# Attention of a four-layer graph kernel: the head sums of the softmax made by another engine and another operation

## The reference

```python
q = (x @ Wq + bq).reshape(N, H, HEAD)   # k and v likewise
scores = jnp.einsum('nhd,mhd->nhm', q, k) / np.sqrt(HEAD)
scores = jnp.where(adj[:, None, :] == 0, -1000000000.0, scores)
attn = jax.nn.softmax(scores, axis=1)
attn_out = jnp.einsum('nhm,mhd->nhd', attn, v).reshape(N, D_OUT)
attn_out = attn_out @ Wo + bo
h1 = _layer_norm(x + attn_out, g1, be1)
```

## Time and profile before

| | before |
|---|---|
| median of 3 runs | 468.87 us (468.62 to 468.89) |
| profiled execution | 468.27 us, span 466.5 us |
| granted TensorE clock, mean | 0.996 |
| TensorE matmuls | 449.2 us busy, 96% of the span |
| VectorE | 310.3 us, 67% |
| ScalarE | 191.1 us, 41% |
| GpSimd | 150.9 us, 32% |
| the chain that ended last | PE 80%, DVE 12% |

### The profile page before, as it was taken

One profiled execution on the slowest core, in us unless ns is written; L12 is line 12 of the kernel. 1 busy time (PEld: TensorE's weight loads), 2 busy tenths in 40 slices (PEclk: granted clock), 3 DMA queues, 4 the chain that ended last, 5 costly groups with the idle time before them and its releaser, 6 DMA issues.

```text
span 466.5 us, 5948 instructions
## 1 busy us (share of the span) xinstructions
PE 449.2 (96%) x2108; PEld 328.3 (70%) x2108; DVE 310.3 (67%) x571; ACT 191.1 (41%) x266; POOL 150.9 (32%) x101
## 2 busy tenths in 40 slices
PE   8999999979899999899999999999999999999997
PEld 3456544434458888678878888888888888888766
DVE  5999868999997998943875836252353237133865
ACT  5898834546124440352632262134303332227240
POOL 5000033212111954464243444044434444344100
PEclk9999999999999999899999999999999999999999
DMA  8870007600000555145020222223221342020002
GB/s 280 173 282 1 1 2 161 109 1 0 1 1 1 139 155 202 24 73 199 1 83 8 91 90 91 90 90 115 90 91 31 118 139 74 22 90 1 0 1 91
DMA packets 24203, 37.49 MB, mean 80 GB/s; under 512 B 5744, under 2 KB 6256, under 8 KB 24176
## 3 DMA queue, kind: packets, MB, share of 16 engines
q1 hardware_dynamic: 21728, 32.80, 21.0%
q0 software_dynamic: 2160, 4.19, 5.3%
q10 hardware_dynamic: 288, 0.13, 0.1%
HBM read 36.07 MB, written 1.05 MB: 80 GB/s over the span
## 4 chain that ended last, share of the span: by engine, by line
PE 80%; DVE 12%; issue 3%; ACT 2%; DVEq 1%; DMA 1%; POOL 0%
PE ps L1257 17%; PE ps L1258 17%; PE ps L1259 17%; PE ps L1319 5%; PE ps L1330 4%; PE ps L1286 3%; PE ps L1285 3%; DVE rsum L963 2%; PE ps L1407 2%; PE ps L1312 2%; DVE e_sb L399 2%; DVE one_src L844 1%; DVE stats L770 1%; PE ps L1270 1%; PE ps L1403 1%
## 5 line engine op out<-in xcount | busy, mean ns | idle before, releaser
L481 POOL TENSOR_TENSOR w_lo<-w_stage,w_hi 128x1024 fp32r<-128x1024 f32 x21 | 52.0, 2477 | 134.1 <-ACT w_hi L567 124.2
L567 ACT ACTIVATE w_hi<-w_stage 128x2048 fp32r<-128x2048 f32 x22 | 42.0, 1909 | 53.4 <-PE ps L1259 53.4
L482 POOL TENSOR_TENSOR w_lo<-w_stage,w_hi 128x1024 fp32r<-128x1024 f32 x21 | 55.2, 2631 | 0.0
L1257 PE MATMUL ps<-w_hi,hid_hi 128*128 128x512 f32 x112 | 43.6, 389 | 0.0
L1258 PE MATMUL ps<-w_lo,hid_hi 128*128 128x512 f32 x112 | 43.6, 389 | 0.0
L1259 PE MATMUL ps<-w_hi,hid_lo 128*128 128x512 f32 x112 | 43.6, 389 | 0.0
L1257 PE MATMUL ps<-T_hi,w_hi 128*128 128x512 f32 (+1 forms) x108 | 39.3, 364 | 0.0
L1259 PE MATMUL ps<-T_hi,w_lo 128*128 128x512 f32 (+1 forms) x108 | 38.6, 358 | 0.0
L1258 PE MATMUL ps<-T_lo,w_hi 128*128 128x512 f32 (+1 forms) x108 | 38.6, 357 | 0.0
L1157 DVE TENSOR_SCALAR tmp<-ps,bl 128x512 f32<-128x512 f32 x16 | 12.0, 749 | 39.9 <-ACT hid_hi L721 39.9
L505 POOL TENSOR_TENSOR rstd<-vareps,scalars 128x1 f32<-128x1 f32 x24 | 16.3, 680 | 61.9 <-DVE vareps L772 61.9
(11 more groups left out here) (239 smaller groups left out, 1013.8 us busy)
## 6 DMA issues: line engine op xcount, KB each, us to landing
w_stage<-in_L_gnn_Wr SPq DMA_DIRECT2D x8, 1024.0 KB, 5.1
w_stage<-in_L_gnn_Wl SPq DMA_DIRECT2D x8, 1024.0 KB, 5.3
w_stage<-in_L_gnn_W SPq DMA_DIRECT2D x5, 1024.0 KB, 5.8
x_sb<-in_x SPq DMA_DIRECT2D x4, 256.0 KB, 3.7
w_q<-in_L_gnn_Wq SPq DMA_DIRECT2D x1, 1024.0 KB, 7.2
w_k<-in_L_gnn_Wk SPq DMA_DIRECT2D x1, 1024.0 KB, 9.7
w_v<-in_L_gnn_Wv SPq DMA_DIRECT2D x1, 1024.0 KB, 5.6
w_o<-in_L_gnn_Wo SPq DMA_DIRECT2D x1, 1024.0 KB, 10.6
```

The lines of the kernel that those rows point to most:

```text
L481: gp.tensor_tensor(w_lo[h][:, 0:2], stage[s][:, 0:2], f32(w_hi[h][:, 0:2]), ALU.subtract)
L482: gp.tensor_tensor(w_lo[h][:, 2:4], stage[s][:, 2:4], f32(w_hi[h][:, 2:4]), ALU.subtract)\
L567: nc.scalar.activation(w_hi[home(u)][:], stage[u % 2][:], ACT.Copy).then_inc(hi_made, 1)
L1257: nc.tensor.matmul(goal, a_hi, b_hi, start=start, stop=False, **kw)
```

## The change

It is confined to the attention.

- GpSimd makes two additions a step, from step 1 on: for each group of 4 heads, heads 0, 1 plus heads 2, 3. It writes them to `pair_sums[i % 2]`, laid out 256 columns by 4 sums, so that one operation's outputs for one head lie 4 floats apart.
- VectorE sums the 4 neighbours of each column with one `tensor_reduce` (`head_sum`). Step 0 stays as it was.
- VectorE's order in a step becomes maxima i+1, product of i-1, sum of i, reciprocal of i.
- The exponentials lie in 4 buffers, and TensorE takes the values of step i-3 at step i, in the places where those of i-2 stood (at step 2 there are none).
- Behind the steps TensorE takes values 5, output tiles 0 and 1, values 6, values 7, and then the first 8 transposes of the count matrix (`count_transposes`), which stood ahead of values 7. `attended_out(0)` on ScalarE moves from step 5 to step 6. The products of step 6 are one operation instead of two.

```diff
--- before.py
+++ after.py
@@ -101,7 +101,7 @@
     k_sb = place("k_sb", [P, PAIRS, N], F32, rQK + MAT)
     v_sb = place("v_sb", [P, NT, D], F32, rQK + 2 * MAT)
     half_sum = place("half_sum", [P, HEADS // 2, HN], F32, rQK + 3 * MAT)
-    pool_sum = place("pool_sum", [P, HEADS // 4, HN], F32, rQK + 3 * MAT + 4 * HN * 4)
+    pair_sums = [place(f"pair_sum{i}", [P, HN, HEADS // 2], F32, rQK + 3 * MAT + (1 - i) * 4 * HN * 4) for i in range(2)]
     ff_hi = place("ff_hi", [P, FT, N], F32R, rQK)
     ff_lo = place("ff_lo", [P, FT, N], F32R, rQK + 2 * MAT)
     R_hi = place("R_hi", [P, NT, D], F32R, rQK)
@@ -111,7 +111,7 @@
 
 
 
-    E_BUFS = 3
+    E_BUFS = 4
     e_bufs = [place(f"e_sb{i}", [P, HEADS, HN], F32, rVZ + i * MAT) for i in range(E_BUFS)]
     c_hi = place("c_hi", [P, NT, N], F32R, rVZ)
     c_lo = place("c_lo", [P, NT, N], F32R, rVZ + MAT)
@@ -283,7 +283,7 @@
         inner_made, part_made, edge_cast, weight_made = (sem("inner_made"), sem("part_made"), sem("edge_cast"),
                                                          sem("weight_made"))
         first_half = sem("first_half")
-        sums_made, rinv_made, pool_half = sem("sums_made"), sem("rinv_made"), sem("pool_half")
+        sums_made, rinv_made, pairs_made = sem("sums_made"), sem("rinv_made"), sem("pairs_made")
         dve = sem("dve")
         pool = sem("pool")
         ln_var = sem("ln_var")
@@ -528,12 +528,14 @@
             add_row("L0_gnn_be2", x_sb, be2_added)
             gp.wait_ge(tr_done, tr_no(T0, NT - 1))
             add_row("L0_gnn_bo", h_sb, bo_added)
-            for i in range(DIRECT, STEPS):
-
-                e = e_bufs[i % E_BUFS]
-                gp.wait_ge(exp_done, 2 * i + 1)
-                gp.wait_ge(sums_made, i)
-                gp.tensor_tensor(pool_sum[:], e[:, 0:2], e[:, 2:4], ALU.add).then_inc(pool_half, 1)
+            for i in range(1, STEPS):
+
+                e, pairs = e_bufs[i % E_BUFS], pair_sums[i % 2]
+                gp.wait_ge(sums_made, max(i - 1, 1))
+                for g in range(2):
+                    gp.wait_ge(exp_done, 2 * i + g + 1)
+                    gp.tensor_tensor(pairs[:, :, 2 * g:2 * g + 2].rearrange("p n h -> p h n"), e[:, 4 * g:4 * g + 2],
+                                     e[:, 4 * g + 2:4 * g + 4], ALU.add).then_inc(pairs_made, 1)
             rstd_of(LN1)
             gp.wait_ge(h_ready, NT)
             split_lo(W1B)
@@ -660,7 +662,7 @@
                     coarse_scores(1, 0)
                 if DIRECT <= i + 1 < STEPS:
                     coarse_scores(i + 1, 1)
-                if i == NT + 1:
+                if i == NT + 2:
                     attended_out(0)
                 if i + 2 < STEPS:
                     coarse_scores(i + 2, 0)
@@ -932,11 +934,10 @@
 
             maxima(0)
             values_in(1)
-            for i in range(STEPS):
-                e = e_bufs[i % E_BUFS]
-                if i == 1 or DIRECT < i < STEPS - 1:
-                    maxima(i + 1)
-                r = rsum[:, i % 2, :]
+
+            def head_sum(i):
+
+                e, r = e_bufs[i % E_BUFS], rsum[:, i % 2, :]
                 if i == 0:
                     v.wait_ge(exp_done, 1)
                     nc.vector.tensor_tensor(half_sum[:, 0:2], e[:, 0:2], e[:, 2:4], ALU.add).then_inc(first_half, 1)
@@ -944,31 +945,42 @@
                     link(nc.vector.tensor_tensor(half_sum[:, 2:4], e[:, 4:6], e[:, 6:8], ALU.add))
                     v.wait_ge(first_half, 1)
                     link(nc.vector.tensor_tensor(half_sum[:, 0:2], half_sum[:, 0:2], half_sum[:, 2:4], ALU.add))
-                elif i < DIRECT:
-                    v.wait_ge(exp_done, 2 * (i + 1))
-                    link(nc.vector.tensor_tensor(half_sum[:], e[:, 0:4], e[:, 4:8], ALU.add))
-                    link(nc.vector.tensor_tensor(half_sum[:, 0:2], half_sum[:, 0:2], half_sum[:, 2:4], ALU.add))
+                    nc.vector.tensor_tensor(r, half_sum[:, 0], half_sum[:, 1], ALU.add).then_inc(sums_made, 1)
                 else:
-                    v.wait_ge(exp_done, 2 * (i + 1))
-                    link(nc.vector.tensor_tensor(half_sum[:, 0:2], e[:, 4:6], e[:, 6:8], ALU.add))
-                    v.wait_ge(pool_half, i - DIRECT + 1)
-                    link(nc.vector.tensor_tensor(half_sum[:, 0:2], half_sum[:, 0:2], pool_sum[:], ALU.add))
-                nc.vector.tensor_tensor(r, half_sum[:, 0], half_sum[:, 1], ALU.add).then_inc(sums_made, 1)
-                if i == 0:
-                    maxima(1)
-                    values_in(2)
-                if i == 1:
-                    values_in(3)
+                    v.wait_ge(pairs_made, 2 * i)
+                    nc.vector.tensor_reduce(r, pair_sums[i % 2][:], AX_X, ALU.add).then_inc(sums_made, 1)
+
+            def head_inverse(i):
+
+                r = rsum[:, i % 2, :]
                 v.wait_ge(sums_made, i + 1)
                 nc.vector.reciprocal(r, r).then_inc(rinv_made, 1)
-                if i == 1:
-                    maxima(DIRECT + 1)
+
+            def normalised(i):
+
                 v.wait_ge(rinv_made, i + 1)
-                if i < STEPS - 2:
+                if i < STEPS - 1:
                     probabilities(nc.vector, i, slice(0, HEADS)).then_inc(prob_done, 2)
                 else:
                     probabilities(nc.vector, i, slice(0, HEADS // 2)).then_inc(prob_done, 1)
                     probabilities(nc.vector, i, slice(HEADS // 2, HEADS)).then_inc(prob_done, 1)
+
+            head_sum(0)
+            maxima(1)
+            values_in(2)
+            head_inverse(0)
+            normalised(0)
+            maxima(2)
+            head_sum(1)
+            values_in(3)
+            head_inverse(1)
+            for i in range(2, STEPS):
+                if i + 1 < STEPS:
+                    maxima(i + 1)
+                normalised(i - 1)
+                head_sum(i)
+                head_inverse(i)
+            normalised(STEPS - 1)
 
 
             g1_row, be1_row = wait_row(GAMMA1), wait_row(BETA1)
@@ -1436,25 +1448,18 @@
             values_part(1, 3)
             values_part(2, 0, 1)
             for i in range(STEPS):
-                if i == STEPS - 1:
-
-                    pe.wait_ge(raw_in["o"], 16)
-                    pe.wait_ge(exp_done, 2 * STEPS - 2)
-                    plain_rows_tile(wo_bank(0), 0, att_sb, w_o, wo_done)
                 centre(i, 0)
                 centre(i, 1)
                 if i == 0:
                     scores(1, 0)
                 if i == 1:
                     values_part(3, 1)
-                if i == 2:
+                if i >= 3:
+                    values(i - 3, 0)
+                if i + 1 < STEPS:
                     scores(i + 1, 1)
-                if i >= 2:
-                    values(i - 2, 0)
-                if i + 1 < STEPS and i != 2:
-                    scores(i + 1, 1)
-                if i >= 2:
-                    values(i - 2, 1)
+                if i >= 3:
+                    values(i - 3, 1)
                 if i + 2 < STEPS:
                     scores(i + 2, 0)
                 if i == 0:
@@ -1462,9 +1467,13 @@
                     values_part(3, 0)
                 if i == 1:
                     values_part(3, 2, 3)
+            values(STEPS - 3, 0)
+            values(STEPS - 3, 1)
+            pe.wait_ge(raw_in["o"], 16)
+            plain_rows_tile(wo_bank(0), 0, att_sb, w_o, wo_done)
+            plain_rows_tile(wo_bank(1), 1, att_sb, w_o, wo_done)
             values(STEPS - 2, 0)
             values(STEPS - 2, 1)
-            plain_rows_tile(wo_bank(1), 1, att_sb, w_o, wo_done)
 
             def count_transposes(src, bank, s, done):
 
@@ -1473,10 +1482,10 @@
                 last.then_inc(done, 1)
 
             pe.wait_ge(exp_done, 2 * STEPS)
+            values(STEPS - 1, 0)
+            values(STEPS - 1, 1)
             for s in C_ROWS[:2]:
                 count_transposes(ct_hi, s, s, c_tr)
-            values(STEPS - 1, 0)
-            values(STEPS - 1, 1)
             pe.wait_ge(att_made, 2)
             plain_rows_tile(wo_bank(2), 2, att_sb, w_o, wo_done)
             for t in range(NT // 2):
```

## The result

| | before | after |
|---|---|---|
| median (runs) | 468.76 us (4; 468.62 to 468.89) | 464.67 us (4; 464.59 to 464.84) |
| profiled execution | 468.27 us, span 466.5 | 464.84 us, span 463.0 |
| ratio | 1 | 0.9918, 95% interval 0.9907 to 0.9929 |

The change is 4.1 us faster. In the profiled executions the difference is 3.43 us. The third output tile, by which the prediction measures the attention, starts at 130.85 instead of 134.03, 3.18 earlier. The first matmul of the next part shifts by the same (142.35 to 139.17). VectorE's last operation starts 3.15 earlier (463.65 to 460.50). So the attention made the gain, and the work behind it handed it on.

A forecast was written before the change was run, and what follows sets the result against it. VectorE was taken to bound the attention's steps (7.36 us, to become 6.53); with step 1's loss and the tail, the third output tile starts 2.2 us earlier: 468.9 - 2.2 = 466.7 us, own range 466.2 to 467.2, full range 465.0 to 472.5.

The forecast's parts named there:

- What bounds the kernel: Attention steps from step 3 on: VectorE limits at 7.36 us a step, the loop without its queue needing 6.33.
- the exclusion: Two-input operations of VectorE and GpSimd exclude each other and take turns; VectorE's one-input reduction and reciprocal take no part.
- X: Time of one GpSimd pair sum with strided output: taken as 1.27 to 1.46 us, at most 2.40.
- Rival 1: GpSimd's pair sums are slow: break-even at X = 1.65, 470.4 us at 1.8, about 476.5 at 2.40; chance 0.27.
- a slow reduction: VectorE's new reduction taking 2.28 us instead of 1.22 would make steps of 7.59 and 470.8 us.
- VectorE's step: Attention from step 3 on: maxima 1.39, product 2.21, reduction 1.26, reciprocal 1.67, together 6.53 us instead of 7.36.
- Step 1: Two pair sums collide with product 0 and maxima 2, making the centring of step 2 1.25 us later.
- Rival 2: Nothing is lost in step 1, so 1.25 us comes back: 465.4 us; chance 0.10.
- The tail: From the last centring to the third output tile, TensorE works without idle time for 16.74 us; tile starts at 131.81.
- Taking the difference from the median: The 2.2 us gain, reckoned on the profiled 468.27, was subtracted from the runs' median, giving 468.9 - 2.2 = 466.7 us.

The follow-up runs named there:

- experiment 3: New kernel with VectorE's product of step i again behind the reciprocal of step i; 474.12 us, 1.0115 to the old kernel.
- experiment 4: New kernel with a third GpSimd pair sum in each step (group 0's made twice); 471.27 us, 1.0063 to the old kernel.
- experiment 5: New kernel with pair sums written head by head, contiguous, so VectorE's reduction reads four values 1 KB apart; 468.83 us, 1.0003 to the old kernel.
- experiment 1: New kernel with step 1's sum made by VectorE alone, GpSimd's pair sums beginning at step 2; 464.00 us, 0.9907 to the old kernel.
- second measurement: The new kernel unchanged, timed again beside the old one: 464.79 us (5 runs) against 468.57 (9 runs), 0.9922.
- experiment 10: Old kernel with the new tail of TensorE's queue and ten matmuls filling the gap ahead of the last centring; 468.96 us, 1.0012 to the old kernel.
- experiment 11: Old kernel with the first group's scores of step 5 computed twice, to fill TensorE's gap at step 4; 468.32 us, 0.9994 to the old kernel.
- experiment 8: New kernel with output tile 0 put back ahead of the last centring; 465.54 us, 0.9935 to the old kernel.
- experiment 9: Old kernel with only the tail of TensorE's queue as in the new one; 470.23 us beside 468.51, 1.0034.

## Why the prediction was right in direction and too small

**What bounds the kernel, and the exclusion: right.** VectorE was the limit of each step from step 3 on and still is. That two-input operations of VectorE and GpSimd take turns was read from the earlier trace rows, and experiments 3 and 4 show it from two sides. It holds for a bf16 maximum and for a product with a broadcast input as well. The Trainium skill ("SBUF — State Buffer", section "Who interferes with whom") has it as one lock held for a whole instruction, which an operation of VectorE with two SBUF inputs needs against a GpSimd operation that reads; the trace agrees (maximum 1.76 instead of 0.63).

**X, the unknown: right, at its lower end.** 1.28 us; the range had been 1.27 to 1.46 and the bound 2.40. Rival 1 is excluded: the strided writes cost 0.02 us (experiment 5). The same rival's other condition, a slow reduction, is real when the stride is on the reading side: 1.95.

**VectorE's step: 6.45, not 6.53.** The parts, start to start, are 1.33 (maxima, taken as 1.39), 2.20, 1.25 and 1.67. The first maximum takes 0.63 when it follows the reciprocal without a wait, where rows 1 had 0.68. Over the steps 3 to 7 that is 0.26 us (25.86 instead of 26.12), and 0.06 more up to the last centring.

**Step 1: the mechanism right, the size too large.** 0.90 lost instead of 1.25: m_bf at 82.17 instead of 82.5. Rival 2, that nothing is lost, was wrong (experiment 1: 0.8). The prediction counted 5.85 us from 76.65 (product 2.2, two pair sums of 1.27, maxima of 0.69 and 0.42), that is, mostly whole durations of operations that take turns. With the durations of the trace it would be 2.29 + 2 x 1.28 + 0.69 + 0.42 = 5.96 us, but from 76.74 to m_bf at 82.17 pass 5.43. The 0.53 between them is 0.13 for each of the four changes of turn, about as much as the start-up that overlaps the end of the operation before; that this is the reason was not tried.

**The tail: 16.43, not 16.74.** Three times 16 values matmuls were taken at 1.88, and the fourth is in the 3.07 read from the old tail, where they stand between other work. Run as 32 in a row they take 3.60 start to start (115.39 to 118.99), 1.80 each, and from the start of values 7 (127.86, half way through the 3.60 from 126.06) to the third tile it is 2.99. With 0.08 four times that is the difference of 0.31, to rounding.

Together they make the third tile 0.96 earlier than forecast: 0.33 at maxima 3 (87.09, not 87.42), 0.26 and 0.06 in the steps, 0.31 in the tail. That is 3.18 us instead of 2.22.

**Taking the difference from the median: the largest single term, and the least certain.** The prediction worked with the profiled execution of before, 468.27, and then subtracted 2.2 from the median 468.87, as if the 0.6 between them belonged to both kernels. They do not: after, the profiled execution lies 0.17 above its median. The medians differ by 4.09 and the profiled executions by 3.43, so 0.66 of the gain is in that step; 0.25 more (3.43 less 3.18) lies behind VectorE's last operation, in the last stores. In the second measurement the medians differ by 3.78 only, by which the 0.66 would be 0.35. Experiments 10 and 11 point to the reason: the old kernel has a gap of 2.05 us at step 4, behind which the clock falls in some executions, and the new kernel's attention has none of that length (its longest is 1.78). The profiled execution of before happened to be one in which it did not fall. The fall is shown in one execution of a kernel with the same gap; that it makes the whole 0.66 is argued, not shown. A gap of 2.02 to 2.03 us that both kernels have further on (before the matmuls at 193.32 in the old one and 190.16 in the new one) does not enter: the clock fell behind it in both profiled executions and not in that of experiment 1, and the work far behind it keeps its distance from the third tile (130.85 to 260.1, 130.08 to 259.3).

In sum 2.2 + 0.96 + 0.25 + 0.66 = 4.1. So what failed is the sizes and not the mechanism. On the path step 1 was taken 0.33 too long, the steps up to the last centring 0.32 and the tail 0.31, and the conversion from the profiled execution to the median left out 0.66. The range's lower end was rival 2's sum with 0.4 of margin; it left no room for several small terms that were all rounded against the change.

**What the tail's reordering is worth.** The prediction counted 2.2 as one sum. Experiment 8 shows 0.8 for the place of tile 0 in the new kernel, and experiment 9 a loss of 1.7 for the same move in the old one. Between the two lie 2.5 us. About half, 1.3, is the clock behind the gap ahead of the last centring, which is 1.78 us with the shorter step and 2.69 with the old one (experiment 10). The rest fits what the tile's old place costs in the new kernel alone: it puts the centring so late that the last pair sums meet product 6 (experiment 8), and the old kernel has no such pair sums. With the gap filled the move gained the old kernel nothing either (468.96 beside 468.65).

The lowest median is that of experiment 1, 464.0 us; its interval overlaps that of the new kernel.

## What to carry to other kernels

Put the stride on the side that does not feel it: here GpSimd's writes took 16-byte steps at a cost of 0.02 us, and VectorE's reduction paid 60% for reading so. When two engines take turns on a resource, order the work by who needs it: pair sums that stood beside one-input operations were free, and the same ones ahead of a maximum cost most of their length (1.76 instead of 0.63 us, for a pair sum of 1.28). Before a stall of TensorE is removed by taking its work away, ask how long the gap becomes; and before a difference is subtracted from a median, look how the profiled execution lies among the runs. A range should leave room for every term of the sum, and not only for the largest rival.

## What the hardware showed that I had not expected

- A gap of TensorE can cost more than itself. After 2.69 us idle the granted clock was 0.50 to 0.55 for 3.5 us (experiment 9); after 1.78 us it stayed at 1.00 (the kernel after); after 2.05 us it stayed at 1.00 in the profiled execution of before and fell to 0.50 in experiment 10. The length alone does not decide: the clock also fell behind 2.07 us (experiment 4) and 3.15 us (experiment 3), and it stayed at 1.00 behind 2.52 us (experiment 5, last centring), 2.60 us (experiment 4, last centring) and 2.92 us (experiment 3, step 3).
- A reduction of 1024 elements in fours takes 1.21 us when they are neighbours and 1.95 when they are 1 KB apart.
- A GpSimd addition with an output step of 16 bytes takes 1.28 us, with a contiguous output 1.26.
